# A graph network of four layers on one core: weights of later linear stages loaded one stage ahead, attention heads divided in the staging, and the sources' one-hot places made by ScalarE

## The reference

```python
# layer 0: filter by edge
h = x @ W_in2f;  Wij = ssp(rbf @ Wf1 + bf1) @ Wf2 + bf2;  Wij = Wij * dist_cut
m = segment_sum(h[idx_j] * Wij, idx_i);  m = ssp(m @ Wo1 + bo1) @ Wo2 + bo2
x = layernorm(x + (x + m))
# layer 1: attention, 8 heads of 32
score = einsum(K[src], Q[dst]) / sqrt(32) + edge_bias
ex = exp(score - segment_max(score, dst)[dst]);  attn = ex / segment_sum(ex, dst)[dst]
out = segment_sum(attn * V[src], dst) @ Wp + bp
h1 = layer_norm(h + out);  h2 = layer_norm(h1 + gelu(h1 @ W1 + b1) @ W2 + b2)
# layer 2: h = x @ W_in + b_in, then three times
h = relu(mean of h[src] by dst @ W_agg[l] + h @ W_self[l] + b_hid[l]);  x = h @ W_out + b_out
# layer 3: two relational convolutions, 8 types of edge, 4 bases
```

## Time and profile before

| | us |
|---|---|
| median of 3 runs (lowest, highest) | 6637.45 (6635.18, 6648.09) |
| profiled execution | 6645.83 |
| its span | 6644.0 |
| DVE's 52 one-hots (L769) | 98.60 to 157.73 |
| POOL's sends by source (L570) | from 99.91 |
| POOL's first send by target (L376) | 680.64 |
| `divide_heads` starts | 3242.49 |

### The profile page before, as it was taken

How to read it: one execution, slowest core, us unless ns; L and a number is a source line. 1 busy time by engine, 2 the same in 40 slices (tenths; PEclk the granted TensorE clock), 3 DMA queues, 4 the chain that set the end, 5 groups by cost and what they waited for, 6 DMA issues and landing times. The chain is left out here.

```text
span 6644.0 us, 75988 instructions
## 1 busy us (share of the span) xinstructions
PE 4254.4 (64%) x20490; PEld 2971.7 (45%) x20491; DVE 3136.9 (47%) x6389; ACT 1817.5 (27%) x4089; POOL 4477.0 (67%) x4302
## 2 busy tenths in 40 slices
PE   3000788888776666567697555555567878885554
PEld 2000566666544454456495333333344445553433
DVE  9500455555458888867635232232234434442223
ACT  1000566666535555367464000000000000000000
POOL 3777777777648888545410777677777757776775
PEclk6555899999888989899899667678789889887776
DMA  3112222222136666545201555555556644444333
GB/s 86 45 53 53 68 72 73 72 72 73 30 117 207 213 210 211 146 137 148 83 1 39 169 162 164 150 161 164 152 180 201 202 132 153 148 147 104 101 99 93
DMA packets 450732, 812.01 MB, mean 122 GB/s; under 512 B 144428, under 2 KB 300041, under 8 KB 443916
## 3 DMA queue, kind: packets, MB, share of 16 engines
q0 software_dynamic: 209664, 564.32, 29.9%
q1 hardware_dynamic: 240780, 244.09, 11.6%
HBM read 650.48 MB, written 157.63 MB: 122 GB/s over the span
## 5 line engine op out<-in xcount | busy, mean ns | idle before, releaser
L1455 POOL DMA_INDIRECT p_rows<-table,idx_s x1320 | 1286.7, 975 | 572.8 <-issue 377.1
L1500 PE MATMUL p_psA<-p_rows,p_hot 128*128 128x256 bf16 (+1 forms) x4840 | 937.5, 360 | 721.5 <-DMA p_rows<-table,idx_s 537.8
L1500 PEld LDWEIGHTS p_psA<-p_rows,p_hot 128*128 128x128 bf16 (+1 forms) x4840 | 642.4, 138 | 989.0 <-issue 837.3
L570 POOL DMA_INDIRECT rec_s<-p_rec_out,p_row_s x416 | 453.9, 1091 | 222.8 <-issue 126.2
L654 PE MATMUL p_psW<-p_wf,p_upto 128*128 128x256 f32 x1760 | 477.2, 432 | 137.8 <-DVE p_upto L803 136.9
L584 POOL DMA_INDIRECT p_space<-h_table,p_space x440 | 473.9, 1077 | 134.1 <-issue 134.1
L1739 POOL DMA_INDIRECT p_kg<-kv_table,edge_d x440 | 424.0, 964 | 189.5 <-issue 110.2
L1455 POOL DMA_INDIRECT p_rows<-rel_table,edge_d x440 | 429.1, 975 | 181.6 <-issue 128.8
L1275 POOL DMA_INDIRECT p_rows<-rel_table,edge_d x440 | 439.1, 998 | 163.0 <-issue 131.3
L1876 DVE TENSOR_REDUCE sums<-p_psM 128x8 f32<-128x1024 f32 x440 | 518.0, 1217 | 4.0 <-PE p_psM L1802 3.3
L376 POOL DMA_INDIRECT rec_d<-edge_d,norm x416 | 409.4, 984 | 155.9 <-issue 126.2
(11 more groups left out here) (342 smaller groups left out, 8825.6 us busy)
## 6 DMA issues: line engine op xcount, KB each, us to landing
v_sorted<-p_kg SPq DMA_DIRECT2D x110, 512.0 KB
p_val<-v_sorted SPq DMA_DIRECT2D x110, 512.0 KB, 3.7
rel_table<-p_o SPq DMA_DIRECT2D x50, 1024.0 KB
p_rows<-table,idx_s POOLq DMA_INDIRECT x1320, 3.1
p_space<-rec_s SPq DMA_DIRECT2D x110, 136.0 KB, 2.1
p_rows<-rel_table,edge_d POOLq DMA_INDIRECT x880, 2.8
p_rec_out<-edge_attr SPq DMA_DIRECT2D x103, 128.0 KB, 2.3
table<-p_o SPq DMA_DIRECT2D x50, 192.0 KB
```

What stands on the lines that cost most here:

```text
L570: pool.indirect_dma_start(g.rec_s_rows, bass.IndirectOffsetOnAxis(ap=row_s[:, n * U + u:n * U + u + 1], axis=0), rec_out[q][:, u, :], None ...
L1455: pool.indirect_dma_start(rows[q][:, u, :], None, table, bass.IndirectOffsetOnAxis(ap=idx(n * U + u), axis=0))\
L1500: step = pe.matmul(psA[:, bass.ds(at[u], D)], hot[q][:, u, :], rows[q][:, u, c * D:(c + 1) * D], start=False, stop=(c == terms - 1), skip_ ...
```

## The change

1. The 52 one-hots are made by ACT (`find_spots`), eight activations `|place - i|` of 128x128 and one `relu(1 - x)` of 128x1024 for each, behind the notes of sends 0 to 51. A third buffer in `upto` holds the distances. DVE goes straight on to the target records, and waits for the 52nd product as before.
2. `linear` takes tiles that are already loaded (`held`, `held_hidden`) and loads for later stages (`ahead`). The first stage loads Wo2 and Wk, Wv, Wq, the value pass Wp, the fourth stage W1, b1 and W2, the fifth W_in. The rows of gain and shift stay in their stage but get a semaphore of their own (`rows_in`), for which only POOL waits. The seventh stage loads its weights itself, as before. `far` of the score pass moves into `sums`.
3. `divide_heads` is gone. In the fourth linear stage DVE takes the maximum and the reciprocal of all denominators first, and then divides each block into `stage` (`divide`, lead 3), in place of ACT's `put`.

```diff
@@ -432,6 +432,7 @@
         m.upto = s.sb("upto", [EP, NB * EC])
         spot = [m.upto[:, q * EIGHT * P // 2:(q + 1) * EIGHT * P // 2].bitcast(BF16).rearrange("p (j n) -> p j n", n=P)
                 for q in range(2)]
+        far = m.upto[:, 2 * EIGHT * P // 2:3 * EIGHT * P // 2].bitcast(BF16).rearrange("p (j n) -> p j n", n=P)
...
@@ -694,8 +695,24 @@
                     act.activation(o[:, :, S_W], edge_w[:, c], ACT.Copy)
                     act.activation(o[:, :, S_IDX].bitcast(I32), g.at_d[:, c], ACT.Copy).then_inc(noted, 1)
+                def find_spots(c):
+                    if c:
+                        act.wait_ge(spotted, c)
+                    for j in range(EIGHT):
+                        at = c * EIGHT + j
+                        step = act.activation(far[:, j, :], g.iota_t[:, 0:P], ACT.Abs, scale=-1.0, bias=place_s[:, at:at + 1])
+                    step.then_inc(measured, 1)
+                    act.wait_ge(measured, c + 1)
+                    if c >= 2:
+                        act.wait_ge(located, c - 1)
+                    act.activation(spot[c % 2], far, ACT.Relu, scale=-1.0, bias=1.0).then_inc(spotted, 1)
                 act.wait_ge(placed, 1)
-                pipelined(act, sends, few, [(0, note)])
+                for n in range(sends):
+                    note(Turn(n // few, n % few, few))
+                    if n < EC // EIGHT:
+                        find_spots(n)
                 act.wait_ge(ready, 1)
                 act.wait_ge(opened, 2)
                 act.wait_ge(w_in, 80)
@@ -763,11 +780,6 @@
                 dve.wait_ge(rest_in, 64)
                 dve.sem_inc(placed, 1)
-                for c in range(EC // EIGHT):
-                    if c >= 2:
-                        dve.wait_ge(located, c - 1)
-                    dve.tensor_tensor(spot[c % 2], bc(g.iota_t[:, 0:P], 1, EIGHT), bc(place_s[:, c * EIGHT:(c + 1) * EIGHT], 2, P),
-                                      ALU.is_equal).then_inc(spotted, 1)
                 link(dve.memset(rec_d[:, :, :], 0))
                 link(dve.tensor_copy(rec_d[:, :, D_SRC], src))
                 link(dve.tensor_copy(rec_d[:, :, D_DST], dst))
...
@@ -925,11 +940,13 @@
                             c0 += piece.shape[1]
                         k0 += k
                 for row, ap in zip(rows, norm or ()):
-                    sp.dma_start(row[:, :], ap.partition_broadcast(P)).then_inc(w_in, 16)
-                if hidden is not None:
+                    sp.dma_start(row[:, :], ap.partition_broadcast(P)).then_inc(rows_in, 16)
+                if hidden is not None and held_hidden is None:
...
+                for to, ap in ahead:
+                    sp.dma_start(to, ap, allow_slow_non_contiguous=len(to.shape) == 2).then_inc(ahead_in, 16)
                 if side is not None:
                     side.load(sp, side_in)
                 if n_loads:
...
@@ -998,9 +1019,10 @@
                     act.wait_ge(exped, t.n + 1)
                     act.activation(soft[t.q][:, :], soft[t.q][:, :], ACT.Ln, scale=0.5, bias=half[:, 0:1]).then_inc(lned, 1)
-                stages = [(3, put)]
+                stages = [(3, put)] * (not heads)
+                if hidden is not None and n_loads:
+                    act.wait_ge(w_in, 16 * n_loads)
                 if hidden is not None:
-                    act.wait_ge(w_in, 16 * n_loads)
                     stages += [(1, gelu)]
                 if func == "ssp":
                     act.preload_act_table_set("natural_log_exp_and_others")
@@ -1029,7 +1051,7 @@
                 if side is not None:
                     side.make(pool, side_in, mixed)
                 if norm:
-                    pool.wait_ge(w_in, 16 * n_loads)
+                    pool.wait_ge(rows_in, 16 * len(rows))
                     pipelined(pool, NB, ring, [(0, gain_and_shift)])
             @block.tensor
@@ -1173,7 +1195,20 @@
                 if norm is not None:
                     dve.memset(eps[:, :], EPS).then_inc(eps_set, 1)
-                steps = [(1 + early, keep)] + [(-1, soft_sum)] * (func == "ssp") + [(-1, part)] * in_parts
+                def divide(t):
+                    wait(dve, turned, t.n - (ring - 1))
+                    a, d = (ins[0][:, bass.ds(t.n, 1), c0:c1].rearrange("p o n -> p (o n)") for c0, c1 in ((0, D), (D, D + H)))
+                    dve.tensor_tensor(stage[t.q][:, :].rearrange("p (h d) -> p h d", h=H), a.rearrange("p (h d) -> p h d", h=H),
+                                      bc(d, 2, HD), ALU.mult).then_inc(staged, 1)
+                if heads:
+                    sums = ins[0][:, :, D:D + H]
+                    dve.tensor_scalar(sums, sums, 1e-30, None, ALU.max).then_inc(summed, 1)
+                    dve.wait_ge(summed, 1)
+                    dve.reciprocal(sums, sums).then_inc(ready, 1)
+                    dve.wait_ge(ready, 1)
+                steps = [(3, divide)] * heads + [(1 + early, keep)] + [(-1, soft_sum)] * (func == "ssp") + [(-1, part)] * in_parts
                 steps += [(0, part_queries)] * (cut_into is not None)
                 if norm is not None:
                     steps += [(-1, join), (-2, invert)]
...
@@ -1933,6 +1969,10 @@
                     if n >= VR:
                         sp.wait_ge(summed[U - 1], n - VR + 1)
                     sp.dma_start(val[q][:, :, 0:D], g.v_sorted[:, n * U:(n + 1) * U, :]).then_inc(loaded[q], 16)
+                    if n == VR:
+                        for to, ap in ahead:
+                            sp.dma_start(to, ap).then_inc(ahead_in, 16)
+                sp.wait_ge(ahead_in, 16 * len(ahead))
             @block.scalar
             def _(act):
@@ -2055,20 +2095,6 @@
                     return step
                 unrolled(groups, [(2, join), (2, lower), (0, add(0)), (2, choose_norm), (0, add(1)), (0, add(2)), (0, add(3))])
-def divide_heads(core, g, acc):
-    with core.phase() as s:
-        step = s.sem("step")
-        with core.nc.Block() as block:
-            @block.vector
-            def _(dve):
-                link = chain(dve, step)
-                den, num = acc[:, :, D:D + H], acc[:, :, 0:D].rearrange("p b (h d) -> p b h d", h=H)
-                link(dve.tensor_scalar(den, den, 1e-30, None, ALU.max))
-                link(dve.reciprocal(den, den))
-                link(dve.tensor_tensor(num, num, bc(den, 3, HD), ALU.mult))
 class Relations:
@@ -2243,40 +2269,54 @@
             filter_by_source(core, g, h_table, sums)
         sent = EARLY + BESIDE * (g.NT // U)
         half = (sent + g.EC) // 2
-        with nc.sbuf_tensor("m", [P, g.NB, D], F32) as m:
-            linear(core, g, [sums[:, :, 0:D]], [[w["L0_gnn_Wo1"]]], bias_at["bo1"], "ssp", dst=m,
-                   side=Targets(g, sent, half))
-            linear(core, g, [m[:, :, :]], [[w["L0_gnn_Wo2"]]], bias_at["bo2"], dst=g.x, plus=[(g.x, 2.0)], norm=(),
-                   side=Targets(g, half, g.EC))
+        def pieces(tile, *weights):
+            for n, ap in enumerate(weights):
+                yield tile[:, :, n * D:(n + 1) * D], ap.rearrange("(k p) n -> p k n", p=P)
+        w_p = sb("w_p", [P, KT, D])
         with nc.sbuf_tensor("score", [P, g.NT, H], F32) as score, \
                 nc.sbuf_tensor("type_hot", [P, g.NT, R], BF16) as type_hot:
             with nc.sbuf_tensor("q_parts", [P, g.NB, PARTS * D], BF16) as q_parts, \
                     nc.sbuf_tensor("digits", [P, WORDS], BF16) as digits, \
                     nc.sbuf_tensor("by_node", [P, H, WORDS], BF16) as by_node:
-                linear(core, g, [g.x[:, :, :]], [[w["L1_gnn_Wk"], w["L1_gnn_Wv"], w["L1_gnn_Wq"]]],
-                       tables=[kv_table], side=Digits(g, digits, by_node), cut_into=q_parts)
+                with nc.sbuf_tensor("w_kvq", [P, KT, 3 * D], F32) as w_kvq:
+                    with nc.sbuf_tensor("m", [P, g.NB, D], F32) as m, nc.sbuf_tensor("w_o2", [P, KT, D], F32) as w_o2:
+                        linear(core, g, [sums[:, :, 0:D]], [[w["L0_gnn_Wo1"]]], bias_at["bo1"], "ssp", dst=m,
+                               side=Targets(g, sent, half), ahead=[
+                                   *pieces(w_o2, w["L0_gnn_Wo2"]),
+                                   *pieces(w_kvq, w["L1_gnn_Wk"], w["L1_gnn_Wv"], w["L1_gnn_Wq"])])
+                        linear(core, g, [m[:, :, :]], [[w["L0_gnn_Wo2"]]], bias_at["bo2"], dst=g.x, plus=[(g.x, 2.0)],
+                               norm=(), side=Targets(g, half, g.EC), held=w_o2)
+                    linear(core, g, [g.x[:, :, :]], [[w["L1_gnn_Wk"], w["L1_gnn_Wv"], w["L1_gnn_Wq"]]],
+                           tables=[kv_table], side=Digits(g, digits, by_node), cut_into=q_parts, held=w_kvq)
                 score_pass(core, g, sums, q_parts, kv_table, score, type_hot, digits[:, :], by_node)
-            value_pass(core, g, sums, score, type_hot)
+            value_pass(core, g, sums, score, type_hot, [*pieces(w_p, w["L1_gnn_Wp"])])
         big = [sb(f"big{n}", [P, g.NB, D]) for n in range(2)]
```

(21 more changed lines are left out.)

29 lines of the change are left out of this document (15 added, 14 removed).

## The result

| | before | after |
|---|---|---|
| median of 4 runs (lowest, highest), us | 6638.99 (6635.18, 6648.09) | 6600.72 (6590.16, 6604.50) |
| ratio, 95% interval | | 0.9942 [0.9928, 0.9956] |
| profiled execution, us | 6645.83 | 6604.50 |

The account below looks back on a forecast made before the run. No engine was above 67%: a row of stages with barriers, POOL's first-stage sends paced by DVE's one-hots. 17.3 + 0 + 5.1 + 10.0 + 2.2 + 3.4 = 38.0 us off 6645.83 gives 6607.8, as median 6599.5, range 6583 to 6619.

Parts of the forecast that it names:

- the step from it to the median: Whole kernel: the shown runs' median lies 8.4 us under the profiled execution, so 6607.8 becomes 6599.5.
- The sends: First stage, POOL: without DVE's one-hots 26 sends take 33.0 instead of 58.97 us, 26.0 less before a new wait.
- The new wait: POOL's 17th send, first stage: waits 8.7 us for attribute tile 4, leaving 17.3 us of gain.
- ACT's step: First stage, ACT's one-hots: at most 4.3 us per step, hidden behind POOL's 5.1; cost 0.
- Part 2: Weights loaded one stage ahead: gains 5.1 us in the third linear stage, 10.0 in the fifth, 2.2 in the sixth.
- the second stage: Second linear stage: matmuls start some 2 us earlier, but POOL's 37 sends end it; gain 0, at most 2.
- Part 3: Fourth linear stage: first transpose 12.4 us earlier, less 9 for divisions in the loop; net 3.4 us.
- The collision: Fourth stage's loop: DVE's division waits about 0.4 us for POOL's L1025; net 0.42 us on 21 or so blocks, 9 us.
- the loss that the early loads might have brought: Stages that host the early weight loads: cost 0, at worst 1.5 us where Wo1 shares the queues.
- ACT becomes the pace: Rival, first stage: ACT's step exceeds 5.1 us and POOL waits; at 6.3 us per step, 6661 us; chance 0.03.
- the gain of part 1: First stage, one-hots moved to ACT: 26.0 less 8.7 us of new wait, 17.3 us net; bounds 12 and 26.

Follow-up runs that it names:

- r0_base: The changed kernel with values that PE and ACT load from block plans asserted in bounds; base of the other runs: 6595.66 us, 0.9941 of the kernel before.
- r1: `r0_base` with the 52 one-hots back on DVE, weights and division as changed: 6613.22 us, 0.9962 of the kernel before.
- r7: `r0_base` with one-hots on DVE as eight one-input 128x128 instructions instead of one two-input 128x1024: 7359.02 us, 1.0092 of the kernel before.
- r2: `r0_base` with SP issuing bias rows and five table stores before waiting for the ranking's ends: 6595.77 us, 0.9937 of the kernel before.
- r3: `r0_base` with the division of all 25 blocks a stage of its own again, Wp still loaded ahead: 6595.79 us, 0.9935 of the kernel before.
- r5: `r0_base` with the fourth stage's division made by ACT, eight 128x32 activations per block, instead of DVE: 7270.02 us, 0.9968 of the kernel before.
- r8: `r0_base` run again unchanged, on the third chip: 7277.43 us, 0.9996 of the kernel before.
- r4: `r0_base` with linear stages two, three, five and six loading their own weights again, on the second chip: 7296.31 us, 1.0006 of the kernel before.

## Why the prediction was right

Every term stood within 1.2 us of its rows, and the rest of the 41.2 us, some 3, is no more than the same code scatters between runs (9.5 us in one stretch, see `r0_base`). That the median came within 1.2 us of the forecast is luck beyond that: the profiled execution took 6604.50 us where 6607.8 was worked out, 3.3 less, and the step from it to the median, taken over from before as 8.4 us, was 3.8. The two misses cancel. Point by point:

- *The sends.* 0.97 us from the second one on, 17.3 us less at the first L376. `r1` brings 17.6 back by itself. What costs is the form of DVE's instruction together with its length: of instructions of 0.81 us, two-input ones hold a send up and a one-input one doesn't (L276 and L280 in after), and a held send ends some 0.8 us after the instruction, so that short ones, as in `r7`, cost next to nothing. The pitch of 2.27 us beside the one-hots fits the same rule: it is two of them (59.13 us / 52 = 1.14 us each). The Trainium skill (SBUF — State Buffer, Who interferes with whom) infers that two-input `tensor_tensor` doesn't keep POOL from writing descriptors; the rows of before, of `r1` and of after (1.16 us under L276) disagree. The same section says that such an instruction contends with what POOL reads from SBUF; the send's row numbers are read from there, which would fit, but no run here took them from elsewhere.
- *The new wait.* Foreseen at 8.7 us, measured 9.46 less the usual 0.30, so 9.2. A freed engine reaches the next late thing sooner, and that step was in the sum. `r2` shows its cause.
- *ACT's step* 3.71 us, under POOL's 5.1; the last product at 358.40 against a forecast of 358.
- *Part 2*: 5.2, 10.0 and 3.3 us against 5.1, 10.0 and 2.2. In the second stage the transposes were indeed earlier, and POOL's sends ended it at the same length. The sixth got 1.1 us more than its own wait; the fifth's loop behind its first transpose was 1.0 us shorter, which I take for scatter.
- *Part 3*: 12.4 against 12.4 us, and the period 2.20 where I said 2.28: 9.7 us given back, with 9 forecast. The collision was the one described: the division waits for POOL's gain, the centring no longer waits for the shift. `r3` shows that the division in the loop was worth nothing, and `r5` that its price is DVE's place: elsewhere, 6.6 us come back.
- *Not in the sum*: 2.3 us up to the second linear stage's start, where I had 0 or a loss. From the first stage's first transpose to the second's it took 59.8 us in after, and with the same code there 60.0 in `r1`, 61.1 in `r3` and 63.0 in `r2`: no gain of the change, and no sign of the loss that the early loads might have brought. (For that loss the prediction gives 1.5 us at worst beside a bound of 5.6 less 2.7, which is 2.9.)
- *The rival "ACT becomes the pace"* did not come about on the first chip. On the other two something like it did: ACT stopped within its steps, and by the arithmetic under `r8` the gain of part 1 is missing. The forecast is borne out only for the chip on which the trace of before was taken.

## What to carry to other kernels

When an engine is freed of a slowdown, walk its queue forward at the new pace and look which transfer, issued by an unchanged queue, it now overtakes; here that took a third of what the sends gained (9.2 of 26 us), and moving seventeen issues ahead of an idle wait removed it. Work put between two instructions of other engines that it can collide with is not free in a gap that the average shows: look what runs when it is issued, or give it to an engine that doesn't collide (ACT in `r5`, 6.6 us). Weights that a stage waits for at its start are worth that wait, which can be read beforehand: two of the three stages came out within a tenth of a microsecond, the third within 1.1. And a gain found on one chip (38 us) needn't be there on the next (6 us, not told from nothing).

## What the hardware showed unasked

- Chips differ: the same kernel took 6637 us on one and 7283 and 7294 on two others, with DVE, ACT and POOL busy for the same time (3087, 1984 and 4461 us in `r8`, 3078, 1985 and 4443 in `r0`) and a mean granted TensorE clock of 0.778 against 0.813. Of the 681 us between these two traces, 218 lie ahead of the first linear stage's first transpose, 72 in the first two linear stages, 6 in the third to the sixth with the score and value passes between them, and 385 behind the seventh's first transpose. What the rows show there is DMA (SP's forty fills of L505 take 44.2 us in `r4` instead of 30.4 in after, and in `r8` the second linear stage waited 41.8 us for its last target sends to land, 5.3 in after) and stops called "remote"; what makes the chips differ isn't shown. The end of the second linear stage in `r8`, on POOL:

```profile
2087.84 0.97 POOL L376 DMA_INDIRECT rec_d<-edge_d,norm  x1 [0.30 <-issue]
2130.62 0.21 POOL L2164 MEMSET digits<- 128x128 bf16 x1 [41.81 <-POOLq L80]
```

- A send of POOL that is issued while DVE scans (4.49 us), compares (L242, 2.33 us) or multiplies two tiles (L276, 0.81 us) doesn't go on at a lower speed, but ends 0.8 us after that instruction, however long it is (0.79, 0.84 and 0.85 us in after). Under a `TENSOR_REDUCE` (one input, 0.81 us) and a `MEMSET` (none, 5.89 us) it isn't held, 0.97 us. The DVE instruction loses nothing: the scan takes 4.49 us beside sends and without them.
